# Last task's inverse rows loaded step by step, in a two-layer spectral kernel

## Reference

```python
# first layer
f  = fft2(x, axes=(1, 2), norm='ortho')
Xk = (f.real - f.imag)[:, :, :46]                      # 46 of 90 columns, of which 23 are kept
o1 = relu(einsum('bhwni,nio->bhwno', Xk, w1[0]) + b1[0])
o2 = einsum('bhwni,nio->bhwno', o1, w2[0]) + b2[0]
x  = ifft2(softshrink(o2), s=(45, 90)).real + x
# second layer: the same with complex weights, rfft2 and irfft2
xr, xi = real(xs), imag(xs)
o1r = relu(mm(xr, w1[0]) - mm(xi, w1[1]) + b1[0]);  o1i = relu(mm(xi, w1[0]) + mm(xr, w1[1]) + b1[1])
o2r = softshrink(mm(o1r, w2[0]) - mm(o1i, w2[1]) + b2[0]);  o2i = ...
x  = irfft2(o2r + 1j * o2i, s=(45, 90)) + x
```

## Time and profile before

| | us |
|---|---|
| median of 3 runs | 519.73 (518.99 to 520.14) |
| the profiled execution | 518.5 |
| its span, first to last instruction | 516.7 |
| TensorE busy in it | 475.7 (92%) |
| VectorE, ScalarE, GpSimd busy | 306.7, 209.5, 173.1 |
| mean granted clock of TensorE | 0.971 |

### The profile page before, as it was taken

One profiled execution on the slowest core, in us unless ns is written; L12 is line 12 of the kernel. 1 busy time (PEld: TensorE's weight loads), 2 busy tenths in 40 slices (PEclk: granted clock), 3 DMA queues, 4 the chain that ended last, 5 costly groups with the idle time before them and its releaser, 6 DMA issues.

```text
span 516.7 us, 14864 instructions
## 1 busy us (share of the span) xinstructions
PE 475.7 (92%) x6144; PEld 341.0 (66%) x6144; DVE 306.7 (59%) x674; ACT 209.5 (41%) x473; POOL 173.1 (34%) x194
## 2 busy tenths in 40 slices
PE   3479999999999999999999999999999999998773
PEld 1157787767777677767777776767777777876531
DVE  6534455457754677457754677456764577567643
ACT  0025544643445443543354442554355433434201
POOL 9822313223341344223441244313442123222124
PEclk9859999999999999999999999999999999999967
DMA  8889763667989588977889688977989565644397
GB/s 182 264 229 258 198 192 91 148 204 193 261 230 238 158 229 245 231 207 186 256 238 219 173 198 256 234 201 182 261 222 256 158 176 158 145 100 129 114 257 226
DMA packets 76864, 104.63 MB, mean 203 GB/s; under 512 B 7777, under 2 KB 63319, under 8 KB 76798
## 3 DMA queue, kind: packets, MB, share of 16 engines
q1 hardware_dynamic: 57766, 56.74, 41.1%
q0 software_dynamic: 10608, 40.45, 29.5%
q10 hardware_dynamic: 8424, 6.49, 5.1%
HBM read 52.21 MB, written 51.43 MB: 201 GB/s over the span
## 4 chain that ended last, share of the span: by engine, by line
PE 79%; DVE 6%; DMA 6%; POOL 3%; ACT 2%; issue 2%; SPq 1%; ACTq 1%; POOLq 0%; DVEq 0%
PE ps L620 14%; PE ps L686 13%; PE ps L711 12%; PE ps L673 11%; PE ps L587 10%; PE ps L633 8%; PE ps L698 5%; PE ps L649 4%; PE ps L659 3%; DMA img<-x 2%; DVE img L566 2%; DVE ns L540 2%; POOL xs L384 2%; ACT p L457 1%; DVE nt L518 1%
## 5 line engine op out<-in xcount | busy, mean ns | idle before, releaser
L566 DVE TENSOR_TENSOR img<-ps,img 90x768 f32<-90x768 f32 x92 | 82.6, 900 | 20.3 <-PE ps L620 16.9
L384 POOL TENSOR_TENSOR xs<-xs,nt 128x360 f32<-128x360 f32 (+1 forms) x48 | 41.6, 866 | 147.9 <-DVE nt L518 120.6
L620 PE MATMUL ps<-jr,cst 64*90 64x384 f32 (+1 forms) x358 | 81.5, 525 | 6.7 <-DVE img L566 5.7
L587 PE MATMUL ps<-img,cst 128*64 128x384 f32 (+1 forms) x368 | 70.8, 500 | 9.7 <-DMA img<-x 9.7
L393 POOL DMA_DIRECT2D y<-img x42 | 34.8, 828 | 133.5 <-DVE img L566 133.2
L450 ACT ACTIVATE o<-ps,wt 97x180 f32<-97x180 f32 (+1 forms) x96 | 33.8, 406 | 107.6 <-PE ps L673 107.6
L633 PEld LDWEIGHTS ps<-cst,bt 128*64 128x64 f32 x1472 | 63.2, 141 | 20.4 <-issue 13.9
L540 DVE SCALAR_TENSOR_TENSOR ns<-p,ps 109x384 f32<-109x384 f32 x96 | 53.2, 554 | 37.8 <-ACT p L457 32.9
L633 PE MATMUL ps<-cst,bt 128*64 128x90 f32 x1472 | 69.0, 248 | 6.1 <-DMA bt<-scr_f 6.1
L686 PE MATMUL ps<-wt,o 128*64 128x96 f32 x1472 | 73.9, 249 | 0.2 <-DVE o L532 0.2
L686 PEld LDWEIGHTS ps<-wt,o 128*64 128x64 f32 x1472 | 64.9, 137 | 12.3 <-issue 12.3
(11 more groups left out here) (41 smaller groups left out, 403.0 us busy)
## 6 DMA issues: line engine op xcount, KB each, us to landing
y<-img POOLq DMA_DIRECT2D x35, 540.0 KB, 5.4
img<-x POOLq DMA_DIRECT2D x30, 540.0 KB, 8.3
scr_i<-et SPq DMA_DIRECT2D x48, 270.0 KB, 5.6
scr_f<-fs SPq DMA_DIRECT2D x154, 72.0 KB, 3.3
bt<-scr_f SPq DMA_DIRECT2D x40, 270.0 KB, 5.2
jr<-scr_i SPq DMA_DIRECT2D x48, 216.0 KB, 5.3
img<-x ACTq DMA_DIRECT2D x10, 540.0 KB, 6.9
y<-img SPq DMA_DIRECT2D x11, 270.0 KB, 3.5
```

Source lines behind the costliest of these rows:

```text
L384: nc.gpsimd.tensor_tensor(re, re, nt[s % 2][:, :, 0:kws(s), 0:H], ALU.subtract).then_inc(re_ok, 1)
L566: nc.vector.tensor_tensor(y, p, y, ALU.add).then_inc(i_add, 1)
L587: last = mm(ps[64 * r:64 * r + 64, P3 + g % 2, 0:(b - a) * HC], K["w_fwd"], img[t % IMGS][:, a:b, :].rearrange("p h c -> p (h c)"), start= ...
L620: last = mm(ps[0:W, B0 + r, 0:n], K["w_inv"][64 * r:64 * r + 64, :], set_rows(t, j)[64 * r:64 * r + 64, at, 0:n], start=True, stop=True)
```

## The change

The rows of the last task go to f0, which has been free since the first task: after the store of step i of that task, SP waits until the store of step i - 1 has landed and loads its eight rows (six for the last step) for all groups, with two loads for the groups of four image rows and one for the last image row. Only the last step's rows are loaded behind the steps, by SP and ScalarE. Steps 45 to 48 carry 3, 3, 2 and 2 held groups; the last two (HELD = 10 and up) go to bank pairs P2 and P1. GpSimd adds three groups of the last task instead of four, from two buffers in turn, and ScalarE issues their stores. The padding frequency is no longer stored, so every load of jr, in all tasks, covers 2 * KW = 46 rows instead of 2 * KWP = 48; the products of the last task take 46 rows, those of the others 64 as before (the rest is zero).

```diff
+HELD = 10
-LAST_POOL = (1, 4, 7, 10)
+LAST_POOL = (1, 4, 7)
@@ schedule
-    for s, n in ((NSTEPS - 2, 2), (NSTEPS - 1, 2), (NSTEPS, 3)):
+    for s, n in ((NSTEPS - 3, 3), (NSTEPS - 2, 3), (NSTEPS - 1, 2), (NSTEPS, 2)):
         inv[s], held = held[:n], held[n:]
...
     order += held
-    order += [("rows", TASKS - 1, j) for j in range(len(JSETS))]
+    order.append(("last_rows",))
     order += [("inv", TASKS - 1, g) for g in range(GROUPS)]
@@ helpers
-        def set_rows(t, j):
-
-            if t == TASKS - 1 and j >= JR:
-                return bt[j - JR][:, 0:(JSETS[j][1] - JSETS[j][0]) * 2 * HC].rearrange("p (g c) -> p g c", c=2 * HC)
-            return jr[bank_of(t, j)[0]]
+        def last_rows(i, r):
+
+            k0, k1 = 2 * STEP * i, min(2 * STEP * (i + 1), 2 * KW)
+            rows = scr_i[TASKS - 1].rearrange("k e h c -> (k e) h c")[k0:k1]
+            four = rows[:, 0:H - 1, :].rearrange("q (g r s) c -> q g r (s c)", r=2, s=2)[:, :, r, :]
+            return four, f0[64 * r + k0:64 * r + k1, 0:GROUPS - 1, :], rows[:, H - 1, :], f0[k0:k1, GROUPS - 1, 0:HC]
+
+        def pair_of(t, g):
+
+            if t == TASKS - 1:
+                return (P0, P1, P2, P3)[g % 4]
+            return (P2, P1, P3)[held_no(t, g) % 3] if held_no(t, g) >= 0 else P3
@@ SP
-                    sp.dma_start(scr_i[t][STEP * i:STEP * i + STEP].rearrange("k e h c -> (e h) k c"),
-                                 et[s % 2][0:2 * H, :, :]).then_inc(e_st[s % 2], 16)
+                    sp.dma_start(scr_i[t][STEP * i:STEP * i + kws(s)].rearrange("k e h c -> (e h) k c"),
+                                 et[s % 2][0:2 * H, 0:kws(s), :]).then_inc(e_st[s % 2], 16)
+                    if t == TASKS - 1 and i > 0:
+                        sp.wait_ge(e_st[(s - 1) % 2], 16 * ((s - 1) // 2 + 1))
+                        for r in range(2):
+                            four, to, one, to_one = last_rows(i - 1, r)
+                            sp.dma_start(to, four).then_inc(l_ld[0], 16)
+                        sp.dma_start(to_one, one).then_inc(l_ld[0], 16)
...
-                    rows = scr_i[t].rearrange("k e h c -> (k e) h c")
+                    rows = scr_i[t].rearrange("k e h c -> (k e) h c")[0:2 * KW]
                     if g0 == GROUPS - 1:
-                        sp.dma_start(set_rows(t, j)[0:2 * KWP, 0, 0:HC], rows[:, 4 * g0, :]).then_inc(landed, 16)
+                        sp.dma_start(jr[k][0:2 * KW, 0, 0:HC], rows[:, 4 * g0, :]).then_inc(j_ld[k], 16)
                     else:
                         four = rows[:, 4 * g0:4 * g1, :].rearrange("q (g r s) c -> q g r (s c)", r=2, s=2)
                         for r in range(2):
-                            sp.dma_start(set_rows(t, j)[64 * r:64 * r + 2 * KWP, 0:g1 - g0, :], four[:, :, r, :]).then_inc(landed, 16)
+                            sp.dma_start(jr[k][64 * r:64 * r + 2 * KW, 0:g1 - g0, :], four[:, :, r, :]).then_inc(j_ld[k], 16)
+                if kind == "last_rows":
+                    sp.wait_ge(e_st[(NT - 1) % 2], 16 * ((NT - 1) // 2 + 1))
+                    four, to, one, to_one = last_rows(STEPS - 1, 0)
+                    sp.dma_start(to, four).then_inc(l_ld[0], 16)
+                    sp.dma_start(to_one, one).then_inc(l_ld[0], 16)
@@ ScalarE
+                if kind == "last_rows":
+                    act.wait_ge(e_st[(NT - 1) % 2], 16 * ((NT - 1) // 2 + 1))
+                    four, to, _, _ = last_rows(STEPS - 1, 1)
+                    act.dma_start(to, four).then_inc(l_ld[1], 16)
...
-                    if n > 0:
-                        act.wait_ge(i_pool, n)
-                    nc.scalar.activation(p1[0:W], ps[0:W, B0:B0 + 2, 0:2 * HC], ACT.Copy).then_inc(i_act, 1)
+                    act.wait_ge(e_st[NT % 2], 16 * ((NT - 2) // 2 + 1))
+                    if n > 1:
+                        act.wait_ge(i_pool, n - 1)
+                    p = (p1[0:W], et[NT % 2][0:W].rearrange("p (r s) c -> p r (s c)", r=2))[n % 2]
+                    nc.scalar.activation(p, ps[0:W, B0:B0 + 2, 0:2 * HC], ACT.Copy).then_inc(i_act, 1)
+            b, f = divmod(TASKS - 1, HALVES)
+            for n, g in enumerate(LAST_POOL):
+                h0, h1 = hrows(g)
+                act.wait_ge(i_pool, n + 1)
+                act.dma_start(out[b, h0:h1, :, f * HC:(f + 1) * HC].rearrange("h w c -> w h c"), img[(TASKS - 1) % IMGS][0:W, h0:h1, :]).then_inc(y_last_act, 16)
@@ TensorE, "inv"
+                    if t == TASKS - 1:
+                        if g == 0:
+                            pe.wait_ge(l_ld[0], 16 * (3 * (STEPS - 1) + 2))
+                            pe.wait_ge(l_ld[1], 16)
+                            pe.wait_ge(e_act, NT)
+                            pe.wait_ge(e_dve, NT)
+                        elif g < 4:
+                            users = [m for m in range(HELD, GROUPS) if pair_of(TASKS - 2, m) == B0]
+                            pe.wait_ge(i_add, (TASKS - 2) * GROUPS + (users[-1] if users else HELD - 1) + 1)
...
-                        last = mm(ps[0:W, B0 + r, 0:n], K["w_inv"][64 * r:64 * r + 64, :], set_rows(t, j)[64 * r:64 * r + 64, at, 0:n], start=True, stop=True)
+                        last = mm(ps[0:W, B0 + r, 0:n], K["w_inv"][64 * r:64 * r + live, :], rows[64 * r:64 * r + live, 0:n], start=True, stop=True)
```

More of the change, by code:

```diff
@@ L220, in spectral_layers @@
         j_ld = [sem(f"j{k}_loaded") for k in range(JR)]
-        j_tail = [sem(f"last_set{j}_loaded") for j in range(JR, len(JSETS))]
+        l_ld = [sem(f"last_rows{k}_loaded") for k in range(2)]
+        y_last_act = sem("y_of_last_task_stored_act")
         i_mm, i_add = sem("inv_product"), sem("inv_added")
@@ L240, in rows_landed, with held_no @@
             return sum(16 * set_dmas(m % len(JSETS)) for m in range(k, n + 1, JR))
[L242 to L246 removed]
+        def last_rows(i, r):
[3 more added lines that the diff above has]
+            return four, f0[64 * r + k0:64 * r + k1, 0:GROUPS - 1, :], rows[:, H - 1, :], f0[k0:k1, GROUPS - 1, 0:HC]
+        def held_no(t, g):
+            return g - HELD if t == TASKS - 2 else -1
+        def pair_of(t, g):
+            if t == TASKS - 1:
+                return (P0, P1, P2, P3)[g % 4]
+            return (P2, P1, P3)[held_no(t, g) % 3] if held_no(t, g) >= 0 else P3
         def f_dmas(g):
@@ L322, in _ @@
                     k, used = bank_of(t, j)
-                    landed = j_tail[j - JR] if t == TASKS - 1 and j >= JR else j_ld[k]
                     if j == 0:
@@ L328, in _ @@
                         sp.wait_ge(j_clr, j + 1)
-                    if t == TASKS - 1 and j >= JR:
-                        sp.wait_ge(a_mm, 2 * NT)
-                    elif used:
+                    else:
                         m = t * len(JSETS) + j - JR
@@ L340, in _ @@
                         for r in range(2):
-                            sp.dma_start(set_rows(t, j)[64 * r:64 * r + 2 * KWP, 0:g1 - g0, :], four[:, :, r, :]).then_inc(landed, 16)
-                if kind == "inv" and what[0] == TASKS - 1:
+                            sp.dma_start(jr[k][64 * r:64 * r + 2 * KW, 0:g1 - g0, :], four[:, :, r, :]).then_inc(j_ld[k], 16)
[4 more added lines that the diff above has]
+                    sp.dma_start(to_one, one).then_inc(l_ld[0], 16)
+                if kind == "inv" and what[0] == TASKS - 1 and what[1] not in LAST_POOL:
                     g, (h0, h1), (b, f) = what[1], hrows(what[1]), divmod(TASKS - 1, HALVES)
@@ L345, in _ @@
                     sp.dma_start(out[b, h0:h1, :, f * HC:(f + 1) * HC].rearrange("h w c -> w h c"), img[(TASKS - 1) % IMGS][0:W, h0:h1, :]).then_inc(y_last, 16)
-            sp.wait_ge(y_last, 16 * GROUPS)
+            sp.wait_ge(y_last, 16 * (GROUPS - len(LAST_POOL)))
         @block.gpsimd
@@ L400, in _ @@
                     y = img[t % IMGS][0:W, h0:h1, :].rearrange("p (r s) c -> p r (s c)", r=2)
-                    nc.gpsimd.tensor_tensor(y, p1[0:W], y, ALU.add).then_inc(i_pool, 1)
+                    p = (p1[0:W], et[NT % 2][0:W].rearrange("p (r s) c -> p r (s c)", r=2))[n % 2]
+                    nc.gpsimd.tensor_tensor(y, p, y, ALU.add).then_inc(i_pool, 1)
                 if kind == "load" and what[0] % STEPS == 3 and what[0] // STEPS >= 2:
@@ L558, in _ @@
                     h0, h1 = hrows(g)
-                    B0 = P3 if t < TASKS - 1 else 2 * (g % 4)
+                    B0 = pair_of(t, g)
                     dve.wait_ge(i_mm, t * GROUPS + g + 1)
@@ L592, in _ @@
                     t, g = what
[L593 to L610, removed]
+                    B0, n = pair_of(t, g), held_no(t, g)
+                    if t == TASKS - 1:
+                        if g == 0:
+                            pe.wait_ge(l_ld[0], 16 * (3 * (STEPS - 1) + 2))
+                            pe.wait_ge(l_ld[1], 16)
                             pe.wait_ge(e_act, NT)
                             pe.wait_ge(e_dve, NT)
+                        elif g < 4:
```

(18 more changed lines are left out.)

4 lines of the change are left out of this document (3 added, 1 removed).

## The result

The changed kernel takes 672.83 us (median of 4, 672.24 to 677.19) where the kernel before takes 519.93 beside it (518.99 to 521.73): a ratio of 1.296, with an interval of 1.292 to 1.300. The profiled execution took 672.27 with a span of 670.4, so 153.8 us more than that of the kernel before.

What follows compares the result with a forecast made beforehand. TensorE was taken to bound the kernel, with 79% of the chain. The profiled 518.5 + 148 (stops) + 16 (bt load) + 14 (clock) - 5 (end) = 691.5, and with 1.2 for the median 693 us; range 635 to 815.

Steps and rivals of the forecast that it cites:

- What a 46-row load does: All jr loads: engine count is the largest number up to 16 dividing the rows, so 46 rows get two engines.
- rounding up: Rival for the jr loads: rows rounded up per engine, 46 rows keep 16 engines; 514.7 us, chance 0.13.
- pairs of their own: Rival for the jr loads: another engine pair for each, six run side by side; 530 us, chance 0.04.
- The six stops: Tasks 1 to 6: ScalarE waits 24.6 us longer each for fs stores behind the jr loads, 148 us in all.
- the division by 0.87 for GpSimd's queue: Drain of six jr loads: GpSimd's queue holds 13% of the engines, so 28.2 / 0.87 = 32 us.
- the prediction's own low end: Whole run at 68 ns, no share for the other queue, no clock loss: 6 x 20.4 + 16 - 5, 653 us.
- The packet price of 68 ns: Jr loads on two engines: 68 ns per 1536 B packet, chosen over 92 and 137; six loads take 28.2 us.
- The last task's bt load: Last task: the next bt load stands behind six jr loads, landing at 475 where needed at 458.96; 16 us.
- The clock after the stops: After each of seven stops TensorE's granted clock is 0.50 for a while; 2 us taken each, 14 in all.
- The end: Last task's rows, groups, adds and last store: the end comes at 512.0 against 516.7, a gain of 5 us.
- the bound at the slow clock: Last task's groups with the clock at 0.50 throughout: 11.5 x 1.28 + 0.4 = 15.1 us; gain only 1.7.
- The held groups' 2.3: Steps 45 and 46 cost 1.8 and 0.6 more, step 48 0.1 less; last inverse-H product moves from 487.8 to 490.1.

Runs made afterwards that it cites:

- the kernel with 48 rows: The changed kernel with jr loads of 48 rows again and the last store of a task covering all four frequencies: 524.78 us, ratio 1.011 to the kernel before.

## Why the prediction was right, and where it was off

*What a 46-row load does.* Right as forecast: two engines, shown by the marks, by the slices of one tenth, and by 45 and 47 rows, which fall where the divisors put them. The rows before the change could not tell this from rounding up; the page of the Trainium skill that was cited with them (DMA: Bandwidth & Descriptors, "Why a DMA increments its semaphore by 16 and not by 1") could, and every count measured here, 15, 16, 2 and 1, agrees with it. Six loads stood in the queue and two engines' worth of work was done (13.4% of sixteen), so the loads did not run side by side on pairs of their own; which two engines they were, no row shows.

*The six stops.* Right in kind, a little large: 24.6 us each forecast, 131.0 - 8.0 = 123, so 20.5 each, measured; 148 against 123 is the whole miss of the middle. The term that failed is the division by 0.87 for GpSimd's queue. In the stretch of the drain shown SP's queue is the only one listed, and GpSimd issues no transfer between 252.27 and the end of the stop, so nothing shares the engines. Without it the prediction's own low end had 20.4, and 255.25 + 0.8 + 28.2 + 0.8 = 285.05 is where the copies go on (285.27). The packet price of 68 ns, the choice between 68, 92 and 137, was exact.

*The last task's bt load.* 16 forecast, 14.9 measured. *The clock after the stops.* 14 forecast; TensorE's busy time grew by 18.1 for the same matmuls, of which about 4 lie in the last groups (15.0 busy instead of 10.9). That is 14, an upper bound for what of it lies on the path.

*The end.* Wrong in sign: a gain of 5 forecast, a loss of 5 measured in the kernel with 48 rows (524.78 beside 519.45). Three terms of that sum were mis-sized: the landing of the last store, the landing of the rows behind it, and the clock. The groups were to start 3.2 + 2.6 = 5.8 us after the last product and started 10.9 after it (639.6 to 650.5): the landing that I took from the last store of before was 3.3 for the store itself and 6.6 for the rows behind it. And the clock was to rise after five groups, as in the earlier trace rows, but those were products of 64 rows; the edit that I had costed at nothing, 46 rows in place of 64, kept it low, and the bound at the slow clock was the near one: 15.1 to the last adds, 15.6 measured. The held groups' 2.3 were right.

Together: 123 + 15 + 14 + 4.3 (the end from step 43 on, 2.4 and 30.8 - 28.9) = 156, against 153.8 between the two profiled executions. The 123 are ScalarE's; TensorE's own waits for the copies grew by 116 (116.5 from 0.5), so the terms overlap in part.

## What to carry to other kernels

Before a transfer is trimmed, look at the number that the split over engines divides: two rows of padding fewer here took fourteen of sixteen DMA engines away, and one queue served in order carried the delay to stores and loads that had nothing to do with it. Price a late transfer by what stands behind it and what that releases, then ask what is late next; more buffers moved this stop and did not end it. A smaller operand is not free merely because its columns are the same.

## What the runs showed of the hardware

- SP itself stands while it issues a load that runs on few engines: six loads took 2.79 us to issue on sixteen engines, 17.51 on two and 39.33 on one, so that a later DMA is not even issued. I had forecast a wait in the queue, not at its mouth. Both are there: the fs stores issued from 272.81 let the copies go on only at 285.27.
- The granted clock did not follow TensorE's being busy alone. 15 us without a gap with 46 of 64 rows in use stayed at 0.50 in all four kernels here with such last products. In all six kernels whose last products took 64 rows and whose jr loads had 15 or 16 engines it went to 1.00, 3 to 6 us after the first of them. With loads on one or two engines the 64-row products stand in bursts of about 4 us between waits, and the clock rose in or behind some bursts and not others.
